# Local transformer: the mask of a tile by two matmuls of 128 queries, in place of eight matmuls of 32 queries

## The reference

```python
seq_p = jnp.pad(seq, ((1, 0), (0, 0)), constant_values=-1)
jt = jnp.concatenate([seq_p[:nw], seq_p[1:]], axis=1)
mask = (it < jb) | (it > jb + w) | (jb == -1)
sim = jnp.einsum('bhwie,bhwje->bhwij', bq, bk2) * QK_SCALE
sim = jnp.where(mask, -jnp.finfo(sim.dtype).max, sim)
attn = jax.nn.softmax(sim, -1)
```

## Time and profile before

| | |
|---|---|
| median of 3 runs | 5391.65 us (5387.35 to 5395.55) |
| profiled execution | 5392.81 us, its span 5391.0 us |
| PE matmul busy | 4720.6 us, 88% of the span |
| PE weight load busy | 3338.6 us, 62% |
| DVE, ACT, POOL busy | 3708.4, 2807.9, 2810.1 us |
| mask matmuls (L1145) | 1536, from 249.3 to 3516.3 us |

### The profile page before, as it was taken

One profiled execution on the slowest core, in us unless ns is written; L12 is line 12 of the kernel. 1 busy time (PEld: TensorE's weight loads), 2 busy tenths in 40 slices (PEclk: granted clock), 3 DMA queues, 4 the chain that ended last, 5 costly groups with the idle time before them and its releaser, 6 DMA issues. The chain is left out here.

```text
span 5391.0 us, 143191 instructions
## 1 busy us (share of the span) xinstructions
PE 4720.6 (88%) x57069; PEld 3338.6 (62%) x57103; DVE 3708.4 (69%) x8589; ACT 2807.9 (52%) x6208; POOL 2810.1 (52%) x3349
## 2 busy tenths in 40 slices
PE   7699999999999999999999999955375999845886
PEld 3367676666667767666676667744363667623665
DVE  7677777777777777777777777746725656577443
ACT  2266666666666666666666666621023666641342
POOL 4477776777677767776777777701122333311000
PEclk9799999999999999999999999977587999967898
DMA  0211111111111111111111110000211000010012
GB/s 21 66 35 25 25 35 37 25 25 33 32 29 25 35 31 29 25 35 33 29 25 34 22 28 21 18 24 2 77 52 24 2 2 2 1 25 13 26 29 58
DMA packets 312165, 150.62 MB, mean 28 GB/s; under 512 B 146143, under 2 KB 301004, under 8 KB 311244
## 3 DMA queue, kind: packets, MB, share of 16 engines
q1 hardware_dynamic: 309451, 137.20, 10.5%
q0 software_dynamic: 2048, 4.20, 0.3%
HBM read 101.10 MB, written 27.41 MB: 24 GB/s over the span
## 5 line engine op out<-in xcount | busy, mean ns | idle before, releaser
L1450 POOL TENSOR_TENSOR loc_a<-loc_a,loc_b 128x512 f32<-128x512 f32 x768 | 977.2, 1272 | 598.3 <-DVE loc_b L1526 598.3
L1127 PE MATMUL psum<-loc_wqk,loc_xt 128*128 128x512 f32 x1536 | 837.6, 628 | 12.3 <-DVE loc_b L1526 5.9
L1195 PE MATMUL psum<-loc_m,xn_rows 128*128 128x128 f32 x6144 | 843.7, 280 | 3.8 <-DVE y_rows L1558 2.6
L1475 POOL TENSOR_TENSOR loc_a<-loc_a,loc_rn 128x512 f32<-128x512 f32 x768 | 784.9, 1043 | 0.1
L1195 PEld LDWEIGHTS psum<-loc_m,xn_rows 128*128 128x128 f32 x6144 | 745.6, 192 | 55.9 <-issue 36.0
L1319 ACT ACTIVATE loc_sq<-psum 128x512 f32<-128x512 f32 x768 | 456.1, 594 | 449.6 <-PE psum L1127 443.2
L1522 DVE TENSOR_TENSOR loc_a<-psum,loc_rope 128x512 f32<-128x512 f32 x768 | 523.9, 682 | 174.9 <-ACT loc_sq L1319 161.7
L1356 ACT COPY xn_rows<-psum 128x512 f32<-128x512 f32 x768 | 412.3, 589 | 326.6 <-PE psum L1183 324.3
L1482 POOL TENSOR_TENSOR xn_cols<-xn_cols,loc_rec 128x512 f32<-128x512 f32 x384 | 392.3, 1042 | 307.5 <-DVE loc_rec L1553 307.5
L1135 PEld LDWEIGHTS psum<-ident,loc_a 128*128 128x128 f32 x3072 | 347.7, 142 | 317.9 <-issue 307.1
L1526 DVE TENSOR_TENSOR loc_b<-psum,loc_rope 128x512 f32<-128x512 f32 x768 | 520.8, 678 | 0.0
(11 more groups left out here) (370 smaller groups left out, 8532.2 us busy)
## 6 DMA issues: line engine op xcount, KB each, us to landing
loc_x<-loc_shifted SPq DMA_DIRECT2D x192, 256.0 KB, 4.0
loc_shifted<-y_rows SPq DMA_DIRECT2D x144, 64.0 KB
loc_wqk<-in_L_ffn_Wqkv SPq DMA_DIRECT2D x24, 256.0 KB, 3.8
x_rows<-y_rows SPq DMA_DIRECT2D x96, 64.0 KB
x_rows<-y_rows SPq DMA_DIRECT2D x96, 63.5 KB
moe_w<-in_L_ffn_W SPq DMA_DIRECT2D x16, 256.0 KB, 5.0
l3a_qk<-l3a_rot SPq DMA_DIRECT2D x16, 256.0 KB, 2.1
grp_w<-in_L_ffn_W SPq DMA_DIRECT2D x16, 256.0 KB, 4.2
```

The costliest lines, as they stand in the source:

```text
L1127: nc.tensor.matmul(ring("p", i, unit), xt[:, b % 2, t * P:(t + 1) * P], wqk[:, unit * 512:(unit + 1) * 512], start=True, stop=True).then_i ...
L1195: last = nc.tensor.matmul(y_bank[:, 0:P], u[:, i % 2, h // 2, h % 2, :], m[:, h, :], start=(h == 0), stop=(h == HEADS - 1))
L1450: nc.gpsimd.tensor_tensor(part, part, b_[:, g % 2, :], ALU.add).then_inc(sem["added"], 1)
L1475: nc.gpsimd.tensor_tensor(part, part, rn[:, i % 2, 8 * unit:8 * unit + 8].rearrange("p (h e) -> p h e", e=1).to_broadcast([P, 8, DH]), ALU ...
```

## The change

A tile's mask is written by two matmuls, one for each bank, in place of eight. The pick matrix becomes a row of four 32x32 identities (128 columns), so one product repeats the mask for all four windows. The table now holds the two forms of the mask (open first half, closed first half) on the upper and lower 32 rows of each half of the partitions; the second pick matrix, for a sequence's first tile, takes the closed form for window 0 and the other for windows 1 to 3. Nothing is moved in the order.

```diff
-    mask_window = np.zeros((P, 2, HEADS // 2, 2 * WINDOW), np.float32)
-    pick = np.zeros((P, WINDOW), np.float32)
-    for h in range(2):
-        mask_window[64 * h:64 * h + WINDOW] = np.where(open_, 0.0, NEG).transpose(1, 0, 2)[:, :, None, :]
-        pick[64 * h:64 * h + WINDOW] = np.eye(WINDOW)
-    c["mask_window"], c["window_pick"] = mask_window.reshape(P, 2, HEADS * WINDOW), pick
+    mask_window = np.zeros((2, 2, WINDOW, HEADS // 2, 2 * WINDOW), np.float32)
+    mask_window[:] = np.where(open_, 0.0, NEG)[None, :, :, None, :]
+    pick = np.zeros((2, 2, WINDOW, 2, P // WINDOW, WINDOW), np.float32)
+    for first in range(2):
+        for w in range(P // WINDOW):
+            pick[:, int(first == 1 and w == 0), :, first, w, :] = np.eye(WINDOW)
+    c["mask_window"], c["window_pick"] = mask_window.reshape(P, HEADS * WINDOW), pick.reshape(P, 2, P)
...
-    core.pick = sb("pick", [P, WINDOW], BF16)
-    core.window_mask = sb("window_mask", [P, 2, INNER // 2], BF16)
+    core.pick = sb("pick", [P, 2, P], BF16)
+    core.window_mask = sb("window_mask", [P, INNER // 2], BF16)
...
-                nc.vector.tensor_copy(core.pick[:, :], pick32[:, :]).then_inc(converted, 1)
-                nc.vector.tensor_copy(core.window_mask[:, :, :], mask32[:, :, :]).then_inc(converted, 1)
+                nc.vector.tensor_copy(core.pick[:, :, :], pick32[:, :, :]).then_inc(converted, 1)
+                nc.vector.tensor_copy(core.window_mask[:, :], mask32[:, :]).then_inc(converted, 1)
...
-                    for w in range(WPT):
-                        for h in range(2):
-                            nc.tensor.matmul(score_bank[h][32 * w:32 * w + 32, :], core.pick[64 * h:64 * h + 64, :],
-                                             core.window_mask[64 * h:64 * h + 64, int(t == 0 and w == 0), :], start=True, stop=False,
-                                             skip_group_check=True)
+                    for h in range(2):
+                        nc.tensor.matmul(score_bank[h][:, :], core.pick[64 * h:64 * h + 64, int(t == 0), :],
+                                         core.window_mask[64 * h:64 * h + 64, :], start=True, stop=False, skip_group_check=True)
```

More of the change, by code:

```diff
@@ L839, in local_transformer_tables @@
     with ExitStack() as ctx2:
-        pick32 = ctx2.enter_context(nc.sbuf_tensor("loc_pick32", [P, WINDOW], F32))
-        mask32 = ctx2.enter_context(nc.sbuf_tensor("loc_mask32", [P, 2, INNER // 2], F32))
+        pick32 = ctx2.enter_context(nc.sbuf_tensor("loc_pick32", [P, 2, P], F32))
+        mask32 = ctx2.enter_context(nc.sbuf_tensor("loc_mask32", [P, INNER // 2], F32))
         blank = ctx2.enter_context(nc.sbuf_tensor("loc_blank", [WINDOW + 1, NB, P], F32))
@@ L856, in _ @@
                                  .to_broadcast([P, LAYERS_RUN, DH])).then_inc(rope_loaded, 16)
-                sp.dma_start(pick32[:, :], dram["window_pick"]).then_inc(loaded, 16)
-                sp.dma_start(mask32[:, :, :], dram["mask_window"]).then_inc(loaded, 16)
+                sp.dma_start(pick32[:, :, :], dram["window_pick"]).then_inc(loaded, 16)
+                sp.dma_start(mask32[:, :], dram["mask_window"]).then_inc(loaded, 16)
                 sp.wait_ge(blanked, 1)
```

## The result

The changed kernel's median is 5408.19 us in 8 runs beside 5391.6 for the kernel before, a ratio of 1.0028 with an interval of 1.0017 to 1.0040: 15 us slower, 9 to 22. Run again beside other kernels it gave 5413.57 against 5394.52, ratio 1.0032 (1.0020 to 1.0044), 17 us. Differences in us are taken from the ratio with its interval; the medians themselves lie 17 and 19 us apart. The forecast was 22, with a range of 10 to 38.

A forecast was written before the change was run, and what follows sets the result against it. PE's own sequence of starts was taken to bound the local stage. One more change of shape (0.10 us) plus 0.015 for score weights and rounding, x 192 tiles, gave 22 us more: 5414 us, range 5402 to 5430.

The forecast's parts named there:

- PE sets the pace: Local stage: PE's own sequence of starts bounds it, busy 496 to 498 us of each 500; a tile's change returns 192 times.
- One pass, not eight (1 to 3): Mask: entry step stays, two matmuls share one 0.20 us pass as eight did, wider weights cost +0.01 us; together worth nothing.
- A change of shape ahead of the scores (4): Between mask and first scores: a new change from 64*128 to 64*32 makes PE wait, 0.10 us a tile.
- The rival of no step: Behind the mask: the array goes from halves to eighths without waiting, -4 to +2 us, about 5390; chance 0.09.
- Score weights no longer hidden (5): First scores: their weights no longer load under the mask, +0.01 us a tile, 0.015 with half a digit for rounding.
- The sum: Whole local stage: 0.10 + 0.015 = 0.115 us a tile, x 192 = 22 us slower.
- The rival of fewer instructions: Near the scores: the number of instructions holds PE, so 12 fewer records a tile save 14 us, 5377; chance 0.05.

## Why the prediction was right

**PE sets the pace**: held for the change. Added up over the stage, the time from the first mask to the first score grew by 17.6 us, the first half of the scores by 2.2 and the step into the mask by 0.4, and the second half of the scores, which has the pauses, fell by 2.2: 18.0, as much as the local stage. In some of the other kernels PE waited for DVE or ACT more than before, and there its own order was not all that counted.

**One pass, not eight (1 to 3)**: held. The eight matmuls save nothing by becoming two: the pair overlaps, entry and pass are the same to 0.003 us, and no mask at all is worth 25 us. The weights cost 0.005 us more, where I had 0.01 from bf16 loads elsewhere. The 80 ns more that I had estimated from the Trainium skill's rule in "TensorE: Matmul & The Clock Gate", section "LDWEIGHTS (loading the stationary operand)", don't show. For float32 they do: 0.187 us for the mixing's 128 columns and 0.106 for the scores' 32 (medians of the kernel before).

**A change of shape ahead of the scores (4)**: held, and it is shown rather than argued. The first score's load stands 0.32 us behind the masks' first load, there is idle time ahead of it, the cost goes when the wide mask stands beside the mixing, and comes for the narrow one when that stands there. The rival of no step, for which the trace of before had no row, is out: 64*128 to 64*32 and 64*32 to 64*128 both wait. The Trainium skill, "TensorEngine Tiling (Array Packing)", section "Key Properties", has it that a change of mode drains the engine; the trace agrees, with 0.09 to 0.10 us each. What the first weight load behind the change costs comes on top: 0.015 us for the scores' 32 columns (5), and 0.10 for the float32 loads of 128 columns of the output projection, as the kernel with heads 8 and 9 moved showed.

**Score weights no longer hidden (5)**: held. The first half went from 0.773 to 0.788 us, the 0.015 of the sum with its rounding.

**The sum**: 0.115 us a tile was forecast, 0.111 measured, 21.3 us and not 22. The time rose by 15 to 17. What was mis-sized is an implied term, that all of it arrives: between first and last mask it is 19.5 us in one profile and 16.1 in the other. The pauses at block boundaries are part of that: 6.1 us in 2220 before, 4.6 and 3.3 after, so 2 to 4 us of the stage. That 12 records less and 0.1 us more beside the scores make these fewer fits the other kernels, but it was not tried apart from the rest; the other few us (-3.4 and -0.6 in stages that the change doesn't touch) are within scatter.

**The rival of fewer instructions** was rejected for the right row (scores start one pass behind the mask) and yet had something in it: where an operation falls in the count of instructions does matter around the scores, by blocks of 256 and not by each one's issue.

## What to carry to other kernels

Small matmuls that run side by side in parts of the array cost one pass together; count passes and changes of array shape, not matmuls, and put an operation beside others of its own shape. Before moving work on the engine that sets the pace, look at what it hides where it stands: here ACT's copies, DVE's rotation and the program's own supply each turned an expected gain of 4 to 40 us into a loss or cut it. Merging the eight matmuls gained nothing where they stood. Moved beside an operation of its own shape the merged form lost its cost, and it gained 12 to 13 us only together with another move.

## What the runs showed of the hardware that I had not expected

PE pauses at every 256th instruction when a dense part of the program gets there too soon. With the 256 records of a tile's scores together, 1.39 us without a pause, there were 35 pauses of up to 2.1 us in 2220 us (some 130 tiles), 49.6 us in all, and no row names another engine for them: they look like "issue". With the two halves 1.5 us apart, as in the kernel before, they were 6.1 us, and with 0.45 us of other work more between them 0.4. How far ahead of PE the blocks are fetched is open: blocks passed in 2.0 to 2.9 us at the fastest, but pauses also stood in slower ones.

Behind a change of shape the size of the first weight load counts, since it starts with its matmul and not under the work ahead. The scores' load of 32 columns costs 0.015 us there. A float32 load of 128 columns costs 0.10: the output projection's second matmul comes 0.213 us behind its first and not 0.112, and the mixing's second pair 0.313 behind its first and not 0.209 (medians of the kernel before).
